# Layer 2 of a two-layer attention kernel: fewer, longer operand loads, and one transfer that writes two copies

## The reference

```python
qkv = jnp.einsum('ble,fe->blf', x, w_in)
q, k, v = jnp.split(qkv, 3, axis=-1)
q, k, v = (to_heads(q), to_heads(k), to_heads(v))   # 16 heads of 16 features
scores = jnp.einsum('bhqd,bhkd->bhqk', q, k) * scale
scores = scores + alibi_bias(H, L)[None]            # linear in the distance, later keys masked
attn = jax.nn.softmax(scores, axis=-1)
ctx = jnp.einsum('bhqk,bhkd->bhqd', attn, v)
```

## Time and profile before

| what | value |
|---|---|
| time, median of 3 runs | 3677.75 us |
| the profiled execution's own time | 3658.99 us |
| its span, first to last instruction | 3657.2 us |
| TensorE busy | 3449.0 us, 94% of the span |
| VectorE, ScalarE, GpSimd busy | 79%, 68%, 58% of the span |
| mean granted TensorE clock | 0.974 |
| layer 2 | about the last 1850 us |
| moved by the DMA engines | 376.45 MB, mean 103 GB/s |

### The profile page before, as it was taken

One profiled execution on the slowest core, in us unless ns is written; L12 is line 12 of the kernel. 1 busy time (PEld: TensorE's weight loads), 2 busy tenths in 40 slices (PEclk: granted clock), 3 DMA queues, 4 the chain that ended last, 5 costly groups with the idle time before them and its releaser, 6 DMA issues. The chain is left out here.

```text
span 3657.2 us, 79325 instructions
## 1 busy us (share of the span) xinstructions
PE 3449.0 (94%) x26824; PEld 1944.8 (53%) x26824; DVE 2872.1 (79%) x8451; ACT 2484.4 (68%) x5347; POOL 2119.5 (58%) x2340
## 2 busy tenths in 40 slices
PE   5999999999999999999689999999999999999997
PEld 2444444444444444444446666666666666666664
DVE  5899999999998999998267777677777777777773
ACT  2788888788788888887346666566666666666663
POOL 2377777677767777775745455455454554554542
PEclk7999999999999999999879999999999999999997
DMA  4344434433343444343466767767668668677761
GB/s 122 68 83 86 95 68 90 93 87 76 84 99 71 89 88 92 71 87 91 87 130 106 139 120 122 134 118 124 129 120 132 116 120 142 118 121 139 122 108 30
DMA packets 251934, 376.45 MB, mean 103 GB/s; under 512 B 21930, under 2 KB 122448, under 8 KB 251264
## 3 DMA queue, kind: packets, MB, share of 16 engines
q1 hardware_dynamic: 249484, 369.28, 53.2%
q10 hardware_dynamic: 2048, 2.10, 0.4%
HBM read 223.97 MB, written 136.95 MB: 99 GB/s over the span
## 5 line engine op out<-in xcount | busy, mean ns | idle before, releaser
L681 DVE TENSOR_REDUCE maxima<-ps_max 128x1 f32<-128x512 f32 x2048 | 1274.1, 680 | 98.2 <-PE ps_max L444 94.0
L1524 DVE CUSTOM_DVE_ANT_0 ps_max<-ps_max,mask 128x512 f32<-128x512 f32 (+3 forms) x2048 | 962.4, 515 | 353.4 <-PE ps_max L1246 350.7
L575 ACT ACTIVATE probs<-ps_rest 128x512 f32<-128x512 f32 x2048 | 1073.5, 602 | 226.7 <-PE ps_rest L457 224.1
L1397 ACT ACTIVATE probs<-ps_rest 128x512 f32<-128x512 f32 (+3 forms) x2048 | 773.4, 436 | 452.4 <-PE ps_rest L1267 400.0
L444 PE MATMUL ps_max<-k_op,q_op 48*128 48x512 f32 x2048 | 724.5, 446 | 61.8 <-DVE maxima L681 54.0
L457 PE MATMUL ps_rest<-q_op,k_op 50*128 50x512 f32 x2048 | 717.1, 441 | 0.3 <-ACT probs L575 0.2
L444 PEld LDWEIGHTS ps_max<-k_op,q_op 48*128 48x128 f32 x2048 | 340.2, 187 | 531.7 <-DVE maxima L681 411.5
L1246 PE MATMUL ps_max<-k_op,q_op 51*128 51x512 f32 (+3 forms) x2048 | 564.6, 366 | 23.8 <-DVE maxima L1524 4.0
L1267 PE MATMUL ps_rest<-q_op,k_op 53*128 53x512 f32 (+3 forms) x2048 | 559.6, 366 | 19.9 <-DMA q_op<-mrows 19.7
L478 PE MATMUL ps_pv<-probs,v_op 128*32 128x512 f32 x4096 | 543.0, 605 | 1.0 <-ACT oT L587 1.0
L1246 PEld LDWEIGHTS ps_max<-k_op,q_op 51*128 51x128 f32 x2048 | 315.4, 188 | 166.9 <-DVE maxima L1524 89.6
(11 more groups left out here) (145 smaller groups left out, 5465.3 us busy)
## 6 DMA issues: line engine op xcount, KB each, us to landing
qk_parts<-qparts SPq DMA_DIRECT2D x192, 512.0 KB, 3.2
q_op<-qk_parts SPq DMA_DIRECT2D x384, 256.0 KB, 7.8
k_op<-qk_parts SPq DMA_DIRECT2D x192, 256.0 KB, 10.5
xin<-in_x SPq DMA_DIRECT2D x32, 512.0 KB, 4.6
xres<-in_x SPq DMA_DIRECT2D x32, 512.0 KB, 4.8
x_mid<-xo SPq DMA_DIRECT2D x32, 512.0 KB, 3.2
xin<-x_mid SPq DMA_DIRECT2D x32, 512.0 KB, 7.1
xres<-x_mid SPq DMA_DIRECT2D x32, 512.0 KB, 15.8
```

Source lines behind the costliest of these rows:

```text
L575: act.activation(probs[:, quad % 2, at:at + S], ps_rest[:, bank("exp", b, p), :], ACT.Exp).then_inc(ps_out["exp"], 1)
L681: dve.tensor_reduce(at, ps_max[:, bank("max", c, k), :], AX.X, ALU.max).then_inc(ps_out["max"], 1)
L1397: act.activation(probs[quad % 2][:, at:at + nq], ps_rest[:, bank("exp", b, p), 0:nq], ACT.Exp).then_inc(ps_out["exp"], 1)
L1524: dve.tensor_tensor_reduce(row, row, mask[:, S - keys:S], 1.0, LOWEST, ALU.add, ALU.max, at).then_inc(ps_out["max"], 1)
```

## The change

It changes how layer 2's operands are loaded, and the order of the columns of the query and key projections.

- The columns of `wqk1T` are reordered on the host within each block of 128: feature first and head second. So the 128 rows of a stored task are now `(d h)` instead of `(h d)`, and the 8 heads of one feature stand next to each other in DRAM: one operand row is a run of 16 KB, where it was 8 pieces of 2 KB.
- `K_TERMS` is `[1, 0, 0]` instead of `[0, 1, 0]`. The three products are the same three, in another order of the groups. In both operands the two groups with the upper part are now neighbours.
- `load_operands` issues 4 transfers for a unit instead of 6. For the queries and again for the keys there is one of 32 rows (512 KB), which reads the 16 rows of the upper part twice by a leading axis of 2 with step 0, and one of 16 rows (256 KB) with the lower part.
- `UNIT_LOADS` becomes 4 in layer 2; the wait for the end of layer 1's loads is spelled out instead.

```diff
-K_TERMS = [0, 1, 0]
+K_TERMS = [1, 0, 0]
...
-    UNIT_LOADS = 2 * len(Q_TERMS)
+    UNIT_LOADS = 4
...
-                sp.wait_ge(ahead["op_loaded"][unit], 16 * UNIT_LOADS * NB)
+                sp.wait_ge(ahead["op_loaded"][unit], 16 * 2 * len(Q_TERMS) * NB)
...
-            for g in range(len(Q_TERMS)):
-                at = HALF_ROWS * unit + g * DH
-                src = qk_dram[par, Q_TERMS[g], 2 * unit, :, :]
-                sp.dma_start(q_op[at:at + DH, par, :, :].bitcast(F32),
-                             src.rearrange("(h d) s -> d h s", d=DH)).then_inc(op_loaded[unit], 16)
-                src = qk_dram[par, K_TERMS[g], 2 * unit + 1, :, :]
-                sp.dma_start(k_op[at:at + DH, par, :, :].bitcast(F32),
-                             src.rearrange("(h d) s -> d h s", d=DH)).then_inc(op_loaded[unit], 16)
+            top = HALF_ROWS * unit
+            for tile, task, twice, once in ((q_op, 2 * unit, top, top + 2 * DH), (k_op, 2 * unit + 1, top + DH, top)):
+                upper, lower = (qk_dram[par, r, task, :, :].rearrange("(d h) s -> d (h s)", d=DH) for r in range(2))
+                rows = tile[:, par, :, :].bitcast(F32).rearrange("p h s -> p (h s)")
+                sp.dma_start(rows[twice:twice + 2 * DH, :],
+                             upper.unsqueeze(0).to_broadcast([2, DH, HALF * S])).then_inc(op_loaded[unit], 16)
+                sp.dma_start(rows[once:once + DH, :], lower).then_inc(op_loaded[unit], 16)
...
+    w["wqk1T"] = w["wqk1T"].reshape(D, -1, P // DH, DH).transpose(0, 1, 3, 2).reshape(D, -1)
```

## The result

The change made the kernel slower: 3892.91 us against 3677.64 us (medians of four runs each), a ratio of 1.060 with a 95% interval of 1.057 to 1.064. The forecast had the sign and the first step right and the size wrong: it said 4200 us, 522 us more, and it became 215 us.

What follows compares the result with a forecast made beforehand. TensorE, 97% busy, was taken as the bound. Stops for sends and loads lengthen a batch from 55.5 to 73.4 us; 17.9 x 31 = 555, less 34 of today's waits, gives +520, about 4200 us; range 3750 to 4570 us.

Steps and rivals of the forecast that it cites:

- Bound by TensorE, 34.3 us of waits to win at most: Steady layer 2: TensorE 97% busy; its waits for maxima rows, 34.3 us, are the most faster loads can give back.
- Two engines for the long transfers: Operand loads: each 512 KB transfer, its source's outermost axis being the two copies, runs on 2 of 16 engines.
- 10.6 us for 256 KB on one engine, 24.2 us for a group: Operand loads: two long transfers at 10.6 us and two short at 1.5 us keep two engines for 24.2 us.
- I take the whole queue: Sends of maxima rows wait for all loads queued ahead; TensorE stops 4.0 us at quad 1, 13.0 at quad 3.
- The witness for that step: Timeline row before the change: sends issued 0.7 us after group A's first load, still waited for 12.0 us later.
- Rival 1, the sends pass the loads: Only late operand groups count, A by 2.3 us and B by 1.8 us a batch; about 3805 us, chance 0.28.
- The clock: Outside the sum: after each batch's stop, 5 us of TensorE work at half rate would add 155 us.
- Rival 3, all 16 engines: Long operand loads run on 16 engines, a group takes 11.1 us; at best 3644 us, chance 0.10.
- The signs I named: Profile after: 2 small packets per long load, L1179 landings 11 to 13 us minimum, lower DMA share and clock, batch 70 us.

Runs made afterwards that it cites:

- e5: e2 with SP issuing group A only after the maxima rows of quad 1 have landed; 3606.43 us, ratio 0.9835 to the kernel before.
- e1: The change, but the upper part loaded by two transfers of 16 rows, six transfers a unit without the leading axis of 2; 3677.73 us, ratio 1.0055.
- e2: The change, still four transfers a unit, but with the 16 rows outermost on the source side and the copies inside; 3650.15 us, ratio 0.9983.
- e8: The change, but the two transfers of the lower part issued for the first two batches only; 3698.47 us, ratio 1.0090.
- e3: The change, but the keys' upper part goes by two transfers of 16 rows, only the queries' by the one on 2 engines; 3822.57 us, ratio 1.0452.
- e4: The change, but the maxima rows sent for the first two batches only; 3859.12 us, ratio 1.0547.

## Why the prediction was wrong in size

- **Bound by TensorE, 34.3 us of waits to win at most.** Right in substance. The two rows are largely the same waits seen from two sides, so less was to be had. Yet e5 won 57 us: its clock went from 0.99 to 1.00 as well, and I had counted only the waits. Of the 1.4 us that a batch of e5 is shorter, 0.6 us are idle time and 0.8 us busy time.
- **Two engines for the long transfers.** Right, and shown by the count of small packets, by the DMA share of 0.12, and by e1 and e2, where the leading axis is gone and the loss with it. By the rule of the Trainium skill ("DMA: Bandwidth & Descriptors", "Why a DMA increments its semaphore by 16 and not by 1"), the divisor of 2 and 32 is 2 and that of 16 and 32 is 16. The traces agree with both, with 5840 of 5842 packets in the change and a landing of 4.8 us in e2.
- **10.6 us for 256 KB on one engine, 24.2 us for a group.** Right as a sum: 27.4 us forecast for group A, 29.0 measured, and 26.1 against 27.1 for B. In parts, 16 pieces of 0.611 us are 9.8 us, a little less than 10.6; the short transfers were under-priced at 1.5 us each, about 2 by e8's difference. The error showed in e3, where four short ones counted: group B landed in 22.4 us, and without one long transfer and the fixed 1.9 us that leaves some 2.7 us for each.
- **The step that failed: "I take the whole queue".** The forecast let the sends of quad 3 wait for all of group B, 13.0 us of its 17.9 us a batch, and those of quad 1 for A's first two transfers, 4.0 us. In the change the sends of quad 3 land in 6.65 us, against 2.5 us with nothing ahead, and stop TensorE for 2.5 us in 30 batches; those of quad 1 stop it for 21.7 us, 0.7 us a batch. In the batch above, where the send is issued at 2645.87 us, its pieces on idle engines go out at 2647.2 and those on the two busy engines at 2650.3, after seven pieces of 0.611 us have started there (some 5 to 7 over all sends of quads 0, 2 and 3). From then on the sends and the loads take turns, one piece each, while group B lands only 20.0 us after the sends were issued. With e4, where the sends are gone and 199 us of loss stay, this shows that the loads themselves, priced at nothing beside the sends' stops, are the loss.
- **The witness for that step.** The 12.0 us of the earlier trace rows didn't show a wait for the whole queue. By the prediction's own prices what lay ahead, an x load and at most two loads, ends and lands in 1.3 + 2 x 2.3 + 1.9 = 7.8 us; the row is longer than that. Nor does the number of pieces explain it: the sends of quad 1 land in 10.1 us in the kernel before, with 2 KB pieces ahead, and in 10.0 us in e1, with 16 KB pieces. What delays them at the start of a group stays open. The row was carried over to the middle of a group, where only the two engines are busy.
- **Rival 1, the sends pass the loads**, was what happened, priced at 4.1 us a batch and 3805 us (the 34 us of waits, which the forecast took off, were left in here). It came to 4.8 us of idle time and 2.4 us of clock, 3893 us. Its 2.3 us for A were 4.1, since A landed in 29.0 us and not in 27.4, and its 1.8 us for B were 0.8. The clock was named in the prediction as a price beside the sum, up to 5 us a batch; I should have put it into both cases. Behind this rival stands the rule of the Trainium skill ("DMA: Bandwidth & Descriptors", "Queues, rings and completion order") that an engine alternates between the queues after a packet of usually 9 to 17 pieces. The direction agrees, but the sends got in after some 5 to 7 pieces, and then piece by piece. At the start of a group, where the pieces are slow, the sends of quad 1 take 11.4 us.
- **Rival 3, all 16 engines**, is what e2 built. It gave 3650 us, near its 3644. That is 10 us from before in the same session, within what can be told.
- **The signs I named.** Packets, DMA share, waits for the loads at L1245 and the lower clock came. "TensorE waits for mrows most" and "70 us a batch" did not. The landing of L1179 stands in no view; its 16 pieces of 0.611 us on each engine fit the long side.

## What to carry to other kernels

Before a transfer is widened by a repeated source, look at which axis ends up outermost on each side: a copy axis of 2 in front confined 512 KB to 2 of 16 engines, and the same copy axis behind the 16 rows did not. A low DMA share can hide that two engines are full; count the small packets, or look for a share of k/16. When a resource is moved off its limit, test the small transfers that share it: here neither the shorter groups nor sending the small rows first was worth much alone, and together they gave 1.6%.

## What the runs showed of the hardware

- A transfer of [2 copies, 16 rows] into 32 partitions ran on 2 of 16 engines (5840 of 5842 small packets, DMA share 0.12). The same bytes as [16 rows, 2 copies] ran on 16 (e2, landing in 4.8 us at best).
- Six transfers of 256 KB into 16 partitions each follow each other by 2.2 to 2.3 us, with pieces of 2 KB and of 16 KB alike (e1). The piece length that looked like the gain was not the limit.
- Pieces of 16 KB were slow at the start of a group, while all 16 engines loaded rows of the same unit: 0.8 to 2.4 us instead of 0.611 us.
- A small transfer of the other queue went out after some 5 to 7 pieces of 16 KB on a busy engine, and then took turns with them, one piece each.
- The same small transfers cost at most 34 us in the change and 181 us in e3: what a delay costs was set by whether TensorE would have waited anyway.
- With one stop of some 4 us in nearly every batch and shorter ones beside it, the mean clock was 0.95 instead of 0.99, a third of the whole loss.
- Not tried: short pieces on 2 engines. Why some sends wait for more pieces than others is open.
